# Moving work between engines in a fused scan and FP4 feed-forward kernel: group 0 rounded in a PSUM bank, seven units' big numbers on VectorE, four pairs scaled on GpSimd, new orders

## What is computed

```python
def reference(x, ...):                       # x: 4 x 1024 x 128, float32
    xn = layernorm(x, axis=-1)
    # part 1: a complex decaying filter along the 1024 steps, per channel
    phazor = exp((angle * 1j - decay) * scale)
    y = real((conv(xn, phazor ** t * phazor_init) + last_conv * phazor ** (t + 1)) * gate)
    # part 2: a feed-forward with block-wise FP4 rounding (blocks of 16) of every operand
    def fp4(v):
        scale = max(max(abs(v_block)) / 6, 1e-12)
        return nearest_on_grid(v / scale) * scale       # grid 0 .5 1 1.5 2 3 4 6
    h = silu(fp4(xn) @ fp4(w_gate).T) * (fp4(xn) @ fp4(w_up).T)     # 352 wide
    z = fp4(h) @ fp4(w_down).T
    return x + y + z
...
```

## Time and profile before

| | |
|---|---|
| median of 3 runs | 132.06 us (132.04 to 132.09) |
| span of the profiled execution | 131.0 us |
| PE busy | 114.4 us (87%) |
| DVE busy | 106.0 us (81%) |
| POOL busy | 102.4 us (78%) |
| ACT busy | 100.8 us (77%) |

### The profile page before, as it was taken

One profiled execution on the slowest core, in us unless ns is written; L12 is line 12 of the kernel. 1 busy time (PEld: TensorE's weight loads), 2 busy tenths in 40 slices (PEclk: granted clock), 3 DMA queues, 4 the chain that ended last, 5 costly groups with the idle time before them and its releaser, 6 DMA issues. The chain is left out here.

```text
span 131.0 us, 2333 instructions
## 1 busy us (share of the span) xinstructions
PE 114.4 (87%) x657; PEld 86.2 (66%) x657; DVE 106.0 (81%) x217; ACT 100.8 (77%) x198; POOL 102.4 (78%) x145
## 2 busy tenths in 40 slices
PE   3800799999949999999999999999799999999992
PEld 3700355446528777757777887777586888788792
DVE  0867949898699879999879998987699899998610
ACT  4287563998858699997799979876959797939840
POOL 4698998699999989999999998994978499630000
PEclk9985555999995999999999999999999999999999
DMA  3990000000000000002001100200020020020202
GB/s 120 323 343 31 3 0 3 0 3 0 0 0 5 0 0 0 0 9 76 0 0 43 39 5 3 80 0 0 0 80 5 0 80 0 0 85 0 83 0 80
DMA packets 3323, 4.90 MB, mean 37 GB/s; under 512 B 496, under 2 KB 1392, under 8 KB 3312
## 3 DMA queue, kind: packets, MB, share of 16 engines
q1 hardware_dynamic: 3168, 4.77, 10.6%
q10 hardware_dynamic: 144, 0.00, 0.1%
HBM read 2.67 MB, written 2.10 MB: 36 GB/s over the span
## 5 line engine op out<-in xcount | busy, mean ns | idle before, releaser
L1140 PE MATMUL ps_u<-wu_T,xq_T 128*128 128x352 f32 x64 | 24.5, 492 | 2.6 <-DVE hq L1590 2.6
L1125 PE MATMUL ps_g<-wg_T,xq_T 128*128 128x352 f32 x64 | 26.0, 489 | 0.1
L1191 PEld LDWEIGHTS ps_o<-wd_T,hq_T 128*128 128x128 f32 x174 | 23.1, 200 | 2.5 <-issue 0.7
L1191 PE MATMUL ps_o<-wd_T,hq_T 128*128 128x128 f32 x174 | 24.4, 285 | 0.0
L807 ACT COPY hq_T<-ps_h 128x384 f32<-128x384 f32 x32 | 15.2, 474 | 6.9 <-PE ps_h L1159 6.8
L801 ACT ACTIVATE silu<-ps_g 128x352 f32<-128x352 f32 x32 | 14.8, 463 | 3.3 <-PE ps_g L1125 2.9
L1590 DVE TENSOR_TENSOR hq<-ps_u,den 128x704 f32<-128x704 f32 (+1 forms) x17 | 14.2, 833 | 2.7 <-PE ps_u L1147 2.7
L1159 PE MATMUL ps_h<-ident,hq 128*128 128x128 f32 x96 | 16.2, 279 | 0.1
L1140 PEld LDWEIGHTS ps_u<-wu_T,xq_T 128*128 128x128 f32 x64 | 11.4, 200 | 7.1 <-DVE hq L1590 3.1
L1159 PEld LDWEIGHTS ps_h<-ident,hq 128*128 128x128 f32 x96 | 12.1, 145 | 5.1 <-issue 3.4
L1545 DVE TENSOR_TENSOR ps_u<-silu,ps_u 128x704 f32<-128x704 f32 (+1 forms) x17 | 14.3, 841 | 1.4 <-PE ps_u L1140 0.8
(11 more groups left out here) (166 smaller groups left out, 248.8 us busy)
## 6 DMA issues: line engine op xcount, KB each, us to landing
x_all<-x_in SPq DMA_DIRECT2D x8, 256.0 KB, 5.1
out<-x_all SPq DMA_DIRECT2D x7, 256.0 KB, 2.0
w_raw<-w_in SPq DMA_DIRECT2D x2, 192.0 KB, 3.9
out<-x_all SPq DMA_DIRECT2D x4, 64.0 KB, 1.6
w_raw<-w_in SPq DMA_DIRECT2D x1, 176.0 KB, 3.9
par<-params_in ACTq DMA_DIRECT2D x1, 3.5 KB, 3.0
```

The lines of the kernel that those rows point to most:

```text
L1125: pe.matmul(ps_g[:, 0:I], x_cols(t), wg_T[:, :], start=True, stop=True).then_inc(s_gate, 1)
L1140: pe.matmul(slot(q)[:, j, 0:I], x_cols(t), wu_T[:, :], start=True, stop=True).then_inc(s_up, 1)
L1191: m = pe.matmul(out_cols(t), hq_T[t % NHT][:, c * P:(c + 1) * P], wd_T[:, c, :], start=False, stop=(c == NCH - 1), skip_group_check=True)
```

## The change

It moves work between the engines and writes every engine's order anew.

- Group 0 of x is no longer rounded by POOL but in two PSUM banks, as h is: DVE divides (`divide_x`), ACT squares and adds, PE rounds (`round_x`), DVE scales (`scale_x`). Its centring moves from POOL to ACT.
- Groups 1 to 3 are normalised by ACT; POOL keeps groups 4 to 7.
- `big_h` of units 6, 8, 10, 12, 14, 15, 16 is done by DVE. The constants that ACT adds are immediates and no longer columns in SBUF.
- Pairs 4, 6, 8, 10: ACT copies the rounded codes out of the slot as bf16 (`copy_codes`), which frees the slot, and POOL multiplies by the scale (`scale_codes`).
- `turn_xn` writes its transposes into PSUM with a column step of four, so that `copy_xnT` is a plain copy.
- The last three tiles get x by an ACT copy (`open_last`) and no longer by a matmul.
- PE runs matmuls on zeros at the start (`stay_busy`). `sum_parts` still transposes both parts of y for all tiles, as before.

```diff
+    IN_BANK = (0,)
+    XN_ACT = (0, 1, 2, 3)
+    BY_POOL = (4, 6, 8, 10)
+    BIG_DVE = (6, 8, 10, 12, 14, 15, 16)
+    Y_POOL = ()
+    Y_DVE = ()
...
+            def scale_codes(q):
+                pool.wait_ge(s_code, sum(1 for k in BY_POOL if k <= q))
+                pool.wait_ge(s_den, q + 1)
+                if q >= NH:
+                    pool.wait_ge(s_hT, PAIR * (q - NH + 1))
+                c = codes[BY_POOL.index(q) % NC].rearrange("p j (b e) -> p j b e", e=BLK)
+                pool.tensor_tensor(hq_blocks(q), c, pair_scales(den[q % ND]), ALU.mult).then_inc(s_hqp, 1)
...
-                act.copy(in_tiles(xn_T[g % NU]), ps_x[:, :].rearrange("d (j p) -> d j p", j=TG)).then_inc(s_xnTc, 1)
+                act.copy(xn_T[g % NU][:, :], ps_x[:, :]).then_inc(s_xnTc, 1)
...
+            def copy_codes(q):
+                act.wait_ge(s_hr, q + 1)
+                if BY_POOL.index(q) >= NC:
+                    act.wait_ge(s_hqp, BY_POOL.index(q) - NC + 1)
+                act.copy(codes[BY_POOL.index(q) % NC][:, :, :], in_slot(q)).then_inc(s_code, 1)
...
+                act.copy(last_bank(t), x_all[:, t, :]).then_inc(s_open, 1)
...
-                    pe.transpose(ps_o[:, 0:P], ident[:, :], ident[:, :])
+            def stay_busy(n):
+                pe.wait_ge(s_idle, 1)
+                for _ in range(n):
+                    pe.matmul(ps_h[:, :], idle[:, 0:P], idle[:, :], start=True, stop=True)
...
-                    m = pe.transpose(ps_x[:, j * P:(j + 1) * P], xn[g][:, j * D:(j + 1) * D], ident[:, :])
+                    m = pe.matmul(in_tiles(ps_x)[:, j, :], xn[g][:, j * D:(j + 1) * D], ident[:, :],
+                                  start=(j == 0), stop=(j == TG - 1), is_transpose=True, skip_group_check=True)
...
+            def round_x(g, n):
...
+                b = xbig[g % NXB][:, xcols(g, n)]
+                pe.matmul(quarter(g, n), unit[0][:, :], b, start=False, stop=False, skip_group_check=True)
+                pe.matmul(quarter(g, n), unit[1][:, :], b, start=False, stop=True,
...
-                    pe.wait_ge(s_hq, q - 1)
+                    wait_slot_free(pe, q - 2)
...
+            stay_busy(6)
+            open_banks()
+            stay_busy(25)
             round_weight(0)
+            stay_busy(1)
             round_weight(1)
...
+            def divide_x(g, n):
...
+                dve.tensor_tensor(blocks(quarter(g, n)), blocks(src[:, xcols(g, n)]),
+                                  spread(x_inverse(g)[:, xblks(g, n)]), ALU.mult).then_inc(s_pv, 1)
...
+            def big_h(n):
...
+                dve.tensor_scalar(big[n % NB][:, j0:j1, :], sqh[n % 2][:, j0:j1, :], BASE, None,
+                                  ALU.add).then_inc(s_bigv, 1)
```

More of the change, by code:

```diff
@@ L128, in build @@
         hq = [sb(f"hq{k}", [P, PAIR, I]) for k in range(NH)]
+        codes = [sb(f"codes{k}", [P, PAIR, I], BF16) for k in range(NC)]
         hq_T = [sb(f"hq_T{k}", [P, NCH * P]) for k in range(NHT)]
@@ L607, in _ @@
+            demodulate_re(0)
             normalise(5, 3)
-            shift_x(4, 1)
-            shift_back_x(4, 1)
-            scale_x(4, 1)
+            normalise(6, 0)
+            shift_x(2)
+            normalise(6, 1)
+            shift_back_x(2)
+            scale_x(2)
+            demodulate_im(0)
+            divide_x(3)
+            normalise(6, 2)
+            modulate_im(0)
+            shift_x(3)
+            shift_back_x(3)
+            scale_x(3)
+            demodulate_im(1)
+            modulate_re(0)
@@ L611, in _ @@
+            divide_x(4)
+            demodulate_im(2)
+            modulate_im(1)
+            shift_x(4)
+            normalise(6, 3)
+            normalise(7, 0)
+            shift_back_x(4)
+            scale_x(4)
+            scale_codes(4)
+            divide_x(5)
+            demodulate_re(1)
             demodulate_re(2)
+            normalise(7, 1)
+            shift_x(5)
             modulate_re(1)
[L613 to L621, removed]
+            shift_back_x(5)
+            scale_x(5)
+            modulate_im(2)
+            scale_codes(6)
             modulate_re(2)
-            modulate_im(2)
             demodulate_re(3)
+            normalise(7, 2)
+            normalise(7, 3)
+            divide_x(6)
             demodulate_im(3)
-            normalise(7, 0)
-            divide_x(6, 1)
+            demodulate_im(4)
@@ L628, in _ @@
             demodulate_re(4)
[L629 to L633, removed]
+            shift_x(6)
+            shift_back_x(6)
+            scale_x(6)
+            scale_codes(8)
+            divide_x(7)
             modulate_re(3)
+            modulate_re(4)
             modulate_im(3)
-            normalise(7, 2)
-            modulate_re(4)
-            normalise(7, 3)
-            divide_x(7, 1)
@@ L1299, in _ @@
             sum_parts(9)
-            gate_tile(21)
             sum_parts(10)
+            sum_parts(11)
+            up_tile(20)
+            up_tile(21)
+            turn_h(13)
+            gate_tile(22)
+            sum_down(12)
             turn_h(14)
-            sum_parts(11)
-            round_h(8)
+            gate_tile(23)
+            round_h(9)
             turn_h(15)
-            gate_tile(22)
+            sum_down(13)
             turn_xq(6, 1)
-            sum_down(12)
-            up_tile(20)
@@ L1339, in _ @@
-            round_h(11)
-            sum_parts(16)
-            turn_xn(6)
-            sum_down(19)
+            turn_xq(7, 1)
+            up_tile(26)
+            up_tile(27)
+            turn_xn(6)
+            gate_tile(28)
+            sum_parts(16)
+            sum_down(19)
+            turn_h(20)
+            turn_xn(7)
+            round_h(12)
+            turn_h(21)
+            gate_tile(29)
             sum_parts(17)
@@ L1737, in _ @@
             maxima_h(2)
-            scale_h(1)
             scales(2)
@@ L1810, in _ @@
             divide_h(11)
+            scan_re(5, 12)
+            product(12)
             scan_im(5, 12)
-            product(12)
+            scale_h(11)
             maxima_h(12)
```

937 lines of the change are left out of this document (516 added, 421 removed).

## The result

| | before | changed |
|---|---|---|
| executions, us | 132.06, 132.09, 132.04, 132.08 | 126.29, 126.39, 127.42, 132.82 |
| span of the profiled one, us | 131.0 | 124.5 |

The ratio is 0.958 (0.953 to 0.964). The forecast was 129.9 us with a range from 127.4 to 132.9.

What follows compares the result with a forecast made beforehand. It took a start-up of some 46 us bound by chains through all engines, then a stretch bound by PE, DVE 9% behind. 46.2 + 76.6 + 3.7 = 126.5, plus 2.3 and 1.06, gave 129.9 us; range 127.4 to 132.9.

Steps and rivals of the forecast that it cites:

- The start-up, up tile 8 at 46.2: Start-up: first product at 24.3 us, `up_tile(8)` at 46.2 instead of 47.28, 1.1 us sooner; bounds 44 and 48.
- I take the first tiles at half speed: Start-up: despite the zeros, PE's clock falls a few us later than before; four up tiles take 1.2 us each.
- The product-to-up-tile-8 stretch: First product to up tile 8: DVE has 19.1 us of work plus 2.8 of waits, 21.9 in all.
- What would show it: Signs in the trace for right, such as up tile 8 near 46.2, or wrong, such as first product past 25.5.
- Rival 1: Start-up gains more: zeros hold the clock, product at 23, up tile 8 at 44, time 127.7 us; chance 0.17.
- After the cut, 76.6 of work and 3.7 lost: From up tile 8's start to PE's last end: 76.6 us of PE work plus 3.7 lost, previously 4.1 lost.
- worth nothing itself: After up tile 8's start: ACT's savings, including `copy_xnT` from 1.11 to 0.60 us, gain nothing directly, given 11 us slack.
- The wait for POOL: After up tile 8's start: DVE's big number waits for the rest of POOL's operation, on average half of 1.1 us.
- Rival 2: After up tile 8's start: DVE's 69 us of work plus 7.1 of waits leave no gain, 131.9 us; chance 0.12.
- 3 (POOL bound): 60 to 85 us: POOL's rounding of x and codes come late, PE loses 3.6 us, time 133.5; chance 0.13.
- Rival 4: Transposes of xn written with a column step cost 0.22 us for 0.11, giving 133 us; chance 0.08.
- Time over the span: Whole kernel: the measured time lies 1.06 us above the profiled span.

Runs made afterwards that it cites:

- E1: The changed kernel with all matmuls on zeros taken out: 127.2 us, ratio to before 0.953 (0.945 to 0.961).
- E3: The changed kernel with groups 1 to 3 normalised by POOL again: 135.5 us.
- E4: The changed kernel with group 0 of x rounded by POOL again: 133.4 us.
- E9: The changed kernel with all seven big numbers on ACT, and groups 1 to 3 normalised by POOL again: 128.8 us, against 124.8 without the latter.
- E13: The kernel before with groups 1 to 3 normalised by ACT: 137.2 us, ratio 1.034 (1.029 to 1.038).
- E15: The changed kernel with all seven big numbers on ACT, and x of the last three tiles by a matmul again: 125.34 us, against 124.8 without the latter.
- E6: The changed kernel with pairs 4, 6, 8 and 10 scaled by VectorE again: 127.63 us, against 126.6 for the changed kernel's executions without a stall.
- E10: The changed kernel with all seven big numbers on ACT, xn transposed into consecutive columns, ACT's copy reordering: 127.65 us, against 124.8 without the latter two.
- E12: The kernel before with only the change's `turn_xn` and `copy_xnT`: 132.4 us, ratio 1.000 (0.998 to 1.003).
- E11: The changed kernel with all seven big numbers on ACT, and no matmuls on zeros: 126.5 us, against 124.8 with the zeros.

## Why the prediction was wrong, step by step

- **The start-up, up tile 8 at 46.2**: the step that failed; it came at 41.8. 3.4 of the 4.4 us lie ahead of the first product (forecast 24.3, measured 20.88), 1.0 behind it (21.9 forecast, 20.9 measured). The prediction had a nearer number beside it, 21.8 "if DVE never waited", and didn't take it; VectorE did not wait from 8 us to the product.
- **"I take the first tiles at half speed"**: wrong, and with "all four up tiles at half clock behind one another" the reason for the 24.3. The granted clock stood at 1.00, and the first up tile took 0.66 us. What half speed costs in this order is some 1.5 us (E1); the other 1.9 of the 3.4 was wrong even for a kernel without zeros, as E1's clock is back after the first up and gate tile. E3 and E4 show that the first product would wait little for POOL's normalising (0.37 us) and long for its rounding of group 0.
- **The product-to-up-tile-8 stretch**: the direction was right (waits for POOL's normalising go), but for each one removed I put a new one in its place without naming a row for it. Of the 2.8 us of waits VectorE has two left, 0.61 for PE's rounding and 0.17 for the first scan's operand. E9 shows that it is worth 3 us only if the first scan's operand isn't late, E13 that it needs the early statistics.
- **What would show it**: the 1.89 us hole at 37 us and the dip behind it are gone, PE is dense from 42 us, `copy_xnT` takes 0.58, and there is no new dip: right.
- **Rival 1**, "the start-up gains more", is what happened, by the mechanism as written, clock and waits both, though not by its sizes: it had 2.4 us for the clock and the product at 23. I gave it 0.17 and stopped at 44 us and 127.7.
- **After the cut, 76.6 of work and 3.7 lost**: 79.9 measured, so 3.3 lost. Nothing contradicts PE's prices; of the 0.66 for x E15 shows some 0.5. But the sum hides two errors. `copy_xnT` "worth nothing itself" is worth 2.8 us, 2.1 of it after the cut: ACT's 11 us of slack said nothing of the steps in which it is the last to be ready. And VectorE's big numbers, priced at 0.75 a pair with 1.3 as the bound and 3.6 us in all, took 1.2 to 1.5 and 6.3 in all; with them on VectorE the time is 1.8 us longer, and 9 of 28 executions lost over 4 us on top.
- **The wait for POOL**: that VectorE's big number would wait for POOL was right; that it waits for the rest of one operation was not. The sign given for wrong, "a DVE big number over 1.2 us", is what the trace shows.
- **Rival 2 (VectorE bound) and 3 (POOL bound)**: VectorE is busy for 71.4 of 74.2 us and near the bound, which E6 bears out; PE never waited for POOL's codes or x. **Rival 4 (turned writes)**: no. The rule of the Trainium skill (SBUF - State Buffer, section "Door 1: The DMA port swizzle") that patterns in PSUM that aren't contiguous slow matmuls doesn't show here: 272 ns per transpose in both forms.
- **Time over the span**: 1.06 came from one execution. The 13 executions of before beside E1 to E4 have 1.96 to 2.12, and the changed kernel's had 1.8. This is 0.7 us of error, opposite in sign to the rest.

## What to carry over

When a change lets the engine that sets the start-up run without waits, price the landmark from that engine's own work first, and add a wait only with a row that names what will be late. Slack in a busy sum doesn't make an operation free: before calling a shorter copy worth nothing, look at whether it is the last thing ready at some step, and remember that the answer belongs to the order of instructions, not to the copy (E10 against E12). Keep VectorE's SBUF-to-SBUF `tensor_scalar` out of stretches where GpSimd works without a pause.

## What the runs showed of the hardware

- The wait of VectorE for GpSimd (POOL) isn't bounded by one operation. The Trainium skill (SBUF - State Buffer, section "SBUF: two separate sides") says that whichever starts first holds the shared ports for its whole instruction; by that the wait would be at most one POOL operation, 1.3 us. Here it was 5.10 and, in E4, 5.09 us, through four further GpSimd operations up to a gap in that queue; in the changed kernel's trace it was 1.50, in between two operations without a gap.
- `divide_x(0, 0)`, a product of two SBUF operands into PSUM, took 1.37 us beside a POOL operation from 11.14 to 12.41, its twin 0.42:

```profile
11.33 1.37 DVE L1722 TENSOR_TENSOR ps_x<-xc,inv_x 128x256 f32<-128x256 f32 x1
12.62 0.42 DVE L1722 TENSOR_TENSOR ps_o<-xc,inv_x 128x256 f32<-128x256 f32 x1
```

- The granted clock of a page can miss a stretch at 1.2 GHz. In E11 it stands at 1.00 (the number behind POOL's), while a matmul of 256 bf16 columns takes 0.42 us, and in the changed kernel at the same place 0.27. The first matmul of 384 columns takes 0.48 us in E11 and 0.48 in before, where the clock reads 0.50; in the changed kernel it takes 0.33:

```profile
14.00:16.00 2.00, 1.94 (x10) 1.57 (x11) 2.00 (x11) 1.63 (x5) 1.61 (x6) 1.00 0.00 0
```

```profile
14.91 0.42 PE L1216 MATMUL ps_x<-xbig,unit 128*128 128x256 bf16 x1
```

```profile
14.02 0.27 PE L1209 MATMUL ps_x<-xbig,unit 128*128 128x256 bf16 x1
```

- ACT's big number of 704 columns takes 0.80 us with the constant in the instruction, and took 0.88 with it in a column of SBUF; the square, which has no such constant, stayed at 0.76. The changed kernel's groups from 34 us on:

```profile
L870 ACT ACTIVATE sqh<-ps_u 128x704 bf16<-128x704 f32 x13 | 9.8, 758 | 1.2 <-DVE ps_u L1757 1.0
L878 ACT ACTIVATE big<-sqh 128x704 bf16<-128x704 bf16 x8 | 6.4, 800 | 0.0
```
